# One-hots of the sources' places: made once per chunk of edges and fetched from DRAM in each step, in a graph network's counts loop

## The reference, cut to what matters

```python
h = relu(layernorm(x)); x = x + L0(h)    # mean of h[src] over each dst, then a dense layer
h = relu(layernorm(x)); x = x + L1(h)    # three attention layers over the edges
h = relu(layernorm(x)); x = x + L2(h)    # mean, max, min, std of messages over each dst
h = relu(layernorm(x)); x = x + L3(h)    # twice: mean of h[src] over each dst, dense layers
```

## Time and profile before

| | |
|---|---|
| median of three runs | 6377.4 us (6375.4 to 6395.1) |
| profiled execution, its own time | 6355.5 us |
| its span | 6353.5 us |
| busy: PE, DVE, ACT, POOL | 41%, 57%, 42%, 69% of the span |
| counts loop, from its first one-hot | 106.6 to about 1041 us |

### The profile page before, as it was taken

One profiled execution on the slowest core, in us unless ns is written; L12 is line 12 of the kernel. 1 busy time (PEld: TensorE's weight loads), 2 busy tenths in 40 slices (PEclk: granted clock), 3 DMA queues, 4 the chain that ended last, 5 costly groups with the idle time before them and its releaser, 6 DMA issues.

```text
span 6353.5 us, 74225 instructions
## 1 busy us (share of the span) xinstructions
PE 2619.9 (41%) x16765; PEld 1698.8 (27%) x16765; DVE 3628.2 (57%) x10270; ACT 2647.2 (42%) x7239; POOL 4376.2 (69%) x4752
## 2 busy tenths in 40 slices
PE   2666666844444434434443344444310000001799
PEld 1111112433333323333333333333200000000444
DVE  4666666956666665566666566666655555555410
ACT  2444442056666635666662566666311111111200
POOL 3999995067777767777775777777477787876000
PEclk9999999866777766777775677777555555555899
DMA  2222224323333333333332333333246555555266
GB/s 87 87 88 87 88 87 175 134 81 111 111 111 111 110 87 93 110 110 110 110 110 79 99 111 110 111 110 110 64 177 224 208 215 217 216 218 195 82 217 228
DMA packets 322843, 824.24 MB, mean 130 GB/s; under 512 B 87854, under 2 KB 234266, under 8 KB 307806
## 3 DMA queue, kind: packets, MB, share of 16 engines
q1 hardware_dynamic: 220462, 600.45, 24.9%
q0 software_dynamic: 102192, 221.85, 14.7%
HBM read 360.65 MB, written 461.39 MB: 129 GB/s over the span
## 4 chain that ended last, share of the span: by engine, by line
POOL 48%; issue 15%; DMA 10%; PE 9%; DVE 9%; ACT 8%; SPq 1%; DVEq 0%; ACTq 0%; POOLq 0%
POOL big L604 32%; POOL big L563 15%; DMA big<-table,src_win 9%; ACT hT L734 5%; PE psT L847 5%; ACT big L760 1%; PE psY L1031 1%; PE psY L1001 1%; PE psY L949 1%; DVE lane_x L1265 1%; DVE far_b L1444 1%; ACT hT L740 1%; DVE top_b L1447 1%; DMA big<-A_d 1%; DVE big L1490 1%
## 5 line engine op out<-in xcount | busy, mean ns | idle before, releaser
L604 POOL DMA_INDIRECT big<-table,src_win x2968 | 3251.2, 1095 | 969.4 <-issue 848.8
L963 PE MATMUL psY<-big,hT 128*128 128x140 bf16 x12600 | 1216.0, 269 | 1752.9 <-ACT hT L740 1750.3
L963 PEld LDWEIGHTS psY<-big,hT 128*128 128x128 bf16 x12600 | 1061.8, 120 | 1907.5 <-ACT hT L740 1773.4
L734 ACT ACTIVATE hT<-src_bc,node_c 128x128 bf16<-128x128 f16 x4200 | 1292.9, 389 | 70.4 <-DMA src_bc<-pe_src_d 70.1
L563 POOL TENSOR_SCALAR big<-big 128x128 bf16<-128x128 bf16 x1584 | 931.8, 606 | 12.2 <-ACT big L664 12.2
L1479 DVE SCALAR_TENSOR_TENSOR big<-big,keep_win 128x132 f32<-128x132 f32 x2184 | 781.9, 358 | 78.5
L1486 DVE SCALAR_TENSOR_TENSOR big<-big,keep_win 128x256 f32<-128x256 f32 x784 | 374.9, 478 | 555.6 <-ACT big L760 527.9
L740 ACT ACTIVATE hT<-hT 128x640 bf16<-128x640 bf16 x840 | 590.6, 722 | 0.0
L1434 DVE TENSOR_TENSOR e_b<-big 128x56 f32<-128x56 f32 x168 | 36.7, 218 | 886.4 <-DMA big<-table,src_win 877.2
L759 ACT ACTIVATE big<-big 128x896 f32<-128x896 f32 x112 | 106.4, 950 | 984.3 <-DMA big<-table,src_win 984.3
L752 ACT ACTIVATE cw_b<-d_b 128x60 f32<-128x60 f32 x168 | 42.5, 253 | 1079.2 <-DVE d_b L1458 1079.2
(11 more groups left out here) (299 smaller groups left out, 3483.3 us busy)
## 6 DMA issues: line engine op xcount, KB each, us to landing
rows<-big SPq DMA_DIRECT2D x112, 1792.0 KB
rows<-big SPq DMA_DIRECT2D x168, 952.0 KB
big<-A_d SPq DMA_DIRECT2D x18, 6400.0 KB, 19.6
A_d<-big SPq DMA_DIRECT2D x396, 200.0 KB, 1.9
big<-table,src_win POOLq DMA_INDIRECT x2968
src_bc<-pe_src_d SPq DMA_DIRECT2D x168, 32.0 KB
table<-big SPq DMA_DIRECT2D x15, 350.0 KB
big<-A_d SPq DMA_DIRECT2D x3, 1600.0 KB, 6.9
```

Of the source, the lines that this page charges most:

```text
L604: pool.indirect_dma_start(out=rows[:, k, p.gather_at:p.gather_at + p.table_w], out_offset=None, in_=table, in_offset=bass.IndirectOffsetOn ...
L734: ins = nc.scalar.activation(is_src[:, t, P:P + n], src_bc[:, s % 2, 0:n], ACT.Square, bias=node_c[:, t:t + 1], scale=-1.0)
L963: ins = nc.tensor.matmul(psY[k][:, 0:p.table_w], is_src[:, t, k * P:(k + 1) * P], table_s[:, t, c, 0:p.table_w], start=(t == 0 and c == 0) ...
```

## The change

- POOL's loop L557 to L564 goes, with `loT`, the four transposes L892 per group and ACT's copies L664.
- A new tensor in DRAM, `lo_d`, holds the `hot_l` of every chunk: 196 x 128 partitions x 512 bf16, 25.7 MB. DVE makes them in a new part `places`, between `path` and `weights`: 50 instructions, each for up to four chunks, into a ring of three buffers that lie in `hT`. SP stores each batch, and a buffer is made anew when its store has landed.
- For this PE transposes the places directly from `edge_s` (8 matmuls, ahead of the marks), and ACT copies them to `lo_e`. The float16 identity is made earlier.
- `path` also turns the chunk's number of each step to integers, `chunk_row`.
- When all batches are stored, SP fetches the `hot_l` of the first four steps. In each step of its loop, behind the store of A, it reads the chunk's number of the step four further on into a register and issues the fetch of 128 KB into the buffer that is now free. A round of the loop has 12 steps. PE waits for the fetch's semaphore and no longer for POOL.

```diff
+MADE, CB = 3, 4
+        lo_d = nc.dram_tensor("lo_d", (nC, P, GJ * P), BF16).ap()
+        batches = [(a, c, min(CB, CP - c)) for a in range(2) for c in range(0, CP, CB)]
...
             sp.wait_ge(blk_rdy, 1)
-            with sp.Fori(0, STEPS // STATES, 1) as rnd:
-                for z in range(STATES):
-                    sp.wait_ge(state_rdy, rnd * STATES + (z + 1))
-                    to = sp.value_load(blk[0:1, bass.ds(rnd * STATES + z, 1)], min_val=0, max_val=DUMP + STEPS - 1)
+            for k, (a, c, n) in enumerate(batches):
+                sp.wait_ge(made, k + 1)
+                sp.dma_start(lo_d.rearrange("(c a) p w -> a p c w", a=2)[a, :, c:c + n, :],
+                             hot_c[:, k % MADE, 0:n, :, :].rearrange("p c j w -> p c (j w)")).then_inc(made_out[k % MADE], 16)
+            for z in range(MADE):
+                sp.wait_ge(made_out[z], 16 * len(range(z, len(batches), MADE)))
+            sp.wait_ge(chunk_row_rdy, 1)
+
+            def load_hots(t, z):
+                frm = sp.value_load(chunk_row[0:1, t], min_val=0, max_val=nC - 1)
+                sp.dma_start(hot_l[:, z, :, :], lo_d[bass.ds(frm, 1), :, :].rearrange("c p (j w) -> p (c j) w", j=GJ)
+                             ).then_inc(hot_l_in[z], 16)
+
+            for t in range(HOTS):
+                load_hots(slice(t, t + 1), t)
+            turn = STATES * HOTS // 2
+            with sp.Fori(0, STEPS // turn, 1) as rnd:
+                for i in range(turn):
+                    z = i % STATES
+                    sp.wait_ge(state_rdy, rnd * turn + (i + 1))
+                    to = sp.value_load(blk[0:1, bass.ds(rnd * turn + i, 1)], min_val=0, max_val=DUMP + STEPS - 1)
                     sp.dma_start(A_d[bass.ds(to, 1), :, :].rearrange("b p q -> p (b q)"),
                                  state_a[:, z, :]).then_inc(state_out[z], 16)
+                    load_hots(bass.ds(rnd * turn + (i + HOTS), 1), i % HOTS)
+            for z in range(HOTS):
+                sp.wait_ge(hot_l_in[z], 16 * (STEPS // HOTS + 1))
...
-            pool.wait_ge(const_rdy, 9)
-            pool.wait_ge(loT_rdy, 4)
-            for t in range(STEPS):
-                if t >= HOTS:
-                    pool.wait_ge(conv_ps, t - HOTS + 1)
-                for j in range(GJ):
-                    ins = pool.tensor_scalar(hot_l[:, t % HOTS, j, :], iota_l, loT[:, j, t:t + 1], None, ALU.is_equal)
-                ins.then_inc(hot_p, 1)
...
+            for a in range(2):
+                act.wait_ge(lo_ps, a + 1)
+                nc.scalar.copy(lo_e[:, a, :, :], psC[2 + a][:, 0:GJ * CP].rearrange("p (j c) -> p j c", j=GJ)).then_inc(lo_rdy, 1)
             deviations(0)
             normalize(0)
-            for k in range(4):
-                act.wait_ge(loT_ps, k + 1)
-                nc.scalar.copy(loT[:, :, k * P:(k + 1) * P],
-                               psT[1][:].rearrange("p (j t) -> p j t", j=GJ)).then_inc(loT_rdy, 1)
...
             for t in range(STEPS):
-                pe.wait_ge(hot_p, t + 1)
                 pe.wait_ge(hot_v, t + 1)
+                pe.wait_ge(hot_l_in[t % HOTS], 16 * (t // HOTS + 1))
...
+                dve.wait_ge(blk_rdy, 1)
+                link(v.tensor_scalar(blk_t, chunk1, -1.0, None, ALU.add))
+                v.tensor_copy(chunk_row, blk_t).then_inc(chunk_row_rdy, 1)
...
+            def places():
+
+                dve.wait_ge(lo_rdy, 2)
+                for k, (a, c, n) in enumerate(batches):
+                    if k >= MADE:
+                        dve.wait_ge(made_out[k % MADE], 16 * (k // MADE))
+                    v.tensor_tensor(hot_c[:, k % MADE, 0:n, :, :],
+                                    iota_l.unsqueeze(1).unsqueeze(1).broadcast_to([P, n, GJ, P]),
+                                    lo_e[:, a, :, c:c + n].rearrange("p j c -> p c j").unsqueeze(3).broadcast_to([P, n, GJ, P]),
+                                    ALU.is_equal).then_inc(made, 1)
...
             fields()
             path()
+            places()
             weights()
```

More of the change, by code:

```diff
@@ L250, in build @@
         T_c = words(32 * G + QW // 2 + P // 2 + 16, 4)
-        assert 33 * G <= SIDE
+        chunk_row = words(33 * G, G).bitcast(I32)
+        lo_e = words(34 * G, nC * GJ // 2).bitcast(BF16).rearrange("p (a j c) -> p a j c", a=2, j=GJ)
+        assert 34 * G + nC * GJ // 2 <= SIDE
+        hot_c = hT[:].rearrange("p t n -> p (t n)")[:, 0:MADE * CB * GJ * P // 2].bitcast(BF16).rearrange(
+            "p (z c j w) -> p z c j w", z=MADE, c=CB, j=GJ)
+        batches = [(a, c, min(CB, CP - c)) for a in range(2) for c in range(0, CP, CB)]
         hot_q = words(0, HOTS * GJ * QW // 2).bitcast(BF16).rearrange("p (z j q) -> p z j q", z=HOTS, j=GJ)
@@ L256, in build @@
         qT = words(TAB, 4 * G).rearrange("p (j t) -> p j t", j=GJ)
-        loT = words(TAB + 4 * G, 4 * G).rearrange("p (j t) -> p j t", j=GJ)
         assert TAB + 8 * G <= U
@@ L322, in build @@
         marks_rdy, mark_ps, chunk_rdy, chunk_ps = sem("marks_rdy"), sem("mark_ps"), sem("chunk_rdy"), sem("chunk_ps")
+        ident_rdy = sem("ident_rdy")
         blk_rdy, c_rdy, edge_t_in = sem("blk_rdy"), sem("c_rdy"), sem("edge_t_in")
-        q_rdy, qT_ps, loT_ps, qT_rdy, loT_rdy = sem("q_rdy"), sem("qT_ps"), sem("loT_ps"), sem("qT_rdy"), sem("loT_rdy")
-        hot_v, hot_d, hot_s, hot_p = sem("hot_v"), sem("hot_d"), sem("hot_s"), sem("hot_p")
+        q_rdy, qT_ps, qT_rdy = sem("q_rdy"), sem("qT_ps"), sem("qT_rdy")
+        lo_ps, lo_rdy, made, chunk_row_rdy = sem("lo_ps"), sem("lo_rdy"), sem("made"), sem("chunk_row_rdy")
+        made_out = [sem(f"made_out{z}") for z in range(MADE)]
+        hot_l_in = [sem(f"hot_l_in{z}") for z in range(HOTS)]
+        hot_v, hot_d, hot_s = sem("hot_v"), sem("hot_d"), sem("hot_s")
         conv_ps, state_rdy = sem("conv_ps"), sem("state_rdy")
@@ L863, in _ @@
             pe.wait_ge(const_rdy, 9)
+            pe.wait_ge(edge_rdy, 3)
+            pe.wait_ge(ident_rdy, 1)
+            for a in range(2):
+                for j in range(GJ):
+                    ins = nc.tensor.matmul(psC[2 + a][:, j * CP:(j + 1) * CP], edge_s[0:CP, a, 2, j * P:(j + 1) * P],
+                                           ident_h[0:CP, 0:CP], start=True, stop=True)
+                ins.then_inc(lo_ps, 1)
             pe.wait_ge(marks_rdy, 1)
@@ L1136, in path @@
                 dve.wait_ge(const_rdy, 9)
+                v.tensor_copy(ident_h[:], ident[:]).then_inc(ident_rdy, 1)
                 link(v.tensor_copy(pos[:, 0:2], part_i[0].rearrange("p (a e) -> p a e", a=2)[:, :, 0]))
@@ L1143, in path @@
                 ins.then_inc(marks_rdy, 1)
-                v.tensor_copy(ident_h[:], ident[:])
                 dve.wait_ge(mark_ps, 1)
```

## The result

The changed kernel took 6532.7 us (median of four runs, 6524.7 to 6547.5) against 6386.3 us for the kernel before (four runs, 6375.4 to 6401.4): 1.023 times as long, 95% interval 1.020 to 1.026. The forecast was 6557 us, slower than before; the measured time is 24 us under it and inside the range. The profiled execution took 6528.45 us, 172.9 more than that of before (1.027 times).

What follows compares the result with a forecast made beforehand. POOL bounds the loop at 2.353 us a step, and SP would after the change. Prelude 109, loop 70 and tail 1 make +180 us: 6536 us profiled, 6557 us with 22 added for the median; range 6473 to 6638.

Steps and rivals of the forecast that it cites:

- SP's turn bounds the loop: In the counts loop, SP's instructions take 2.53 us a step against POOL's 2.353: 70 us longer over 396 steps.
- The first half: SP's existing work in each loop step: wait, block's number into a register, store of A; 1.32 us.
- the second: SP's added work in each loop step: chunk's number into a register and the fetch's DMA instruction; 1.21 us.
- the loop's tail: Behind the loop SP also waits for the last fetch: about 1 us.
- The prelude: Ahead of the loop, DVE makes and SP stores all chunks' one-hots: the loop starts 109 us later, bounds 76 and 124.
- The conversion to the median: On the whole time: the 22 us between profiled execution and median of before, added to 6536 to give 6557 us.
- Rival (a): In the loop, SP is not the bound and DVE is next at 1.5 us a step: 6148 us; chance 0.09.
- Rival (b): In SP's loop, register loads take 470 ns in both halves, 2.93 us a step: +339, 6716 us; chance 0.04.
- Rival (c): SP bounds the loop at 2.38 us a step or less, with fast batches ahead: +87, 6465 us; chance 0.06.

Runs made afterwards that it cites:

- run 1: The changed kernel with the loop's fetch always taking chunk 0, so no chunk number is loaded into a register: 6283.1 us, 1.88 us a step.
- run 2: The changed kernel with each fetch in the loop taking 32 KB instead of 128, register load and DMA instruction kept: 6517.0 us, 2.50 us a step.
- run 7: The kernel before plus SP's chunk-number register load and an 8 KB DMA in each step: 7724.5 us against 7702.0 on that chip, 2.52 us a step.
- run 9: The kernel of run 3 plus one unused register load in each of SP's turns: 6291.1 us, 1.99 us a step.
- run 10: The kernel of run 3 with the loads of src_i and dst_i moved behind the stores of the one-hots on SP: 6032.7 us, 0.9495 of the kernel before.
- run 3: The changed kernel with POOL instead of SP issuing the fetch, as an indirect DMA: 6055.9 us, 0.952 of the kernel before, 1.37 us a step.
- run 4: The kernel before with POOL doing one of its four comparisons in each step from the fifth on: 5954.3 us, 1.37 us a step.

## Why the prediction held, point by point

- **SP's turn bounds the loop.** Right. The step predicted was 2.53 us, measured 2.50. The first half was priced at 1.32, wake-up and branch of every six steps included, the second at 1.21; a plain turn took 1.26 and 1.18, and the branch and single longer turns add 0.06. Runs 1, 2, 7 and 9 show the cause: take the register load out and the step falls with the bytes unchanged, take bytes out and it stays, put the half into the kernel before and SP's waits vanish, add a load and the step rises by 0.62 us. The term was +71 us with the loop's tail and came out at 58.7: the shorter turn is worth some 11 us, and PE starts 0.84 us after the first one-hot where it took 2.62 with POOL.
- **The prelude.** Predicted +109, measured +110.1. Batches 2.28 us, DVE waiting from 57.7 to 90.19 (predicted 58 to 91), the batches' end at 193.4 (192), then the 15 and 8 us whose cover was gone. That the first store is late by the loads of `src_i` and `dst_i` is shown by run 10: with them out of the way it left SP at 53.4 instead of 72.85 and landed 4.9 us later instead of 17.3. That the second part is one DMA engine's backlog is read from the earlier trace rows, not tested by itself. Of the two rows between which the batch's price was chosen, L1468 gave the right number, 1.1 ns an element, but it could not show the reason. It is a float32 row, and the kernel before has a float32 sum of two inputs read straight that is as slow, 396 elements in 0.57 us (L1151, below). With 0.15 us fixed that is 1.06 ns an element, and L1468's is 1.05. So L1468 is explained by its type alone, and the choice of the slow rate for a bf16 batch was supported by no row. The Trainium skill (VectorE: DVE Perf Modes, "Mode 2×_1P — pack two bf16 into one 32-bit read") supports it, since a repeated element is no step of one; the trace agrees with 2284 ns for 2048 bf16 elements. The batch also compares where the faster bf16 row takes a minimum, so no run here separates the repetition from the operation. Of the kernel before:

```profile
47.47 0.57 DVE L1151 TENSOR_TENSOR big<-big 128x396 f32<-128x396 f32 x1
```

- **The conversion to the median.** This is the step with most of the miss. The sum on the profiled execution gave 6536 us and that execution took 6528.5. (The two smaller misses offset each other in part: the loop's term came out 12 us too large, the prelude 1 us and the part behind the loop 4 us too small.) To it I added the 22 us by which the median of before stood over its profiled execution; the changed kernel's median stands 4 over its own. On the two other chips with the same late stages the kernel before had medians of 6358.1 and 6354.7, about its profiled 6355.5. So the profile was no exception; the four runs on record with the result were high, for a reason that stays open. Against 6355 or so the change costs about 175 us and not 146.
- **Rival (a), DVE next at 1.5 us, 6148 us.** Rightly a rival, since SP had to be shown; but its price was wrong. DVE's one-hots take 318 to 328 ns when POOL is out of the way (362 beside it), and the next bound is 1.3 to 1.37, not 1.5. Run 3 gives what the change could have been worth with the fetch on an idle engine: 6056 us.
- **Rival (b), longer register loads.** Not in the changed kernel: 269 ns median, 278 at most for the block's number. The Trainium skill (DMA: Bandwidth & Descriptors, "Latency and other measured facts") names about 600 ns as the least; 269 ns here says otherwise. Longer loads do occur in other runs: up to 931 ns where the DMA engines were 79% busy (run 3), 355 ns in the median at 56% (run 1), but also 67 over 300 ns at 41% in run 4, while the changed kernel had none in its loop at 40%. So the busy DMA engines that the rival gave as its reason are not shown to be it.
- **Rival (c), SP bound but short.** Neither its 2.38 us a step nor its fast batches came.

## What to carry to other kernels

A queue that only issues DMAs has a turn like any engine, and the busy table does not show it: take the time between two of its waits less the wait itself, and add to it every register load (0.6 us with its register work here) and every DMA instruction (0.34 to 0.43 us here) of a change before believing that a freed engine frees the loop. If a fetch needs an address out of memory in each step, give it to an idle engine; here that turned +2.3% into -4.8%. And work moved ahead of a loop costs its own time (here 112 us of DVE) and, on top, what its stores wait behind somebody else's loads (31 us here, by run 10): look at when the queue comes to the first store, not only at the bytes.

## What the runs showed that I had not expected

- A register load out of SBUF on SP takes 262 to 269 ns and is as long in the median at 79% DMA share (270), but single ones then last up to 931 ns; in run 1 the median itself was 355. In run 4 nearly all the long ones are the first behind the branch of SP's loop, in run 1 none of these is long. What makes a load long is open.
- A DMA instruction with a fixed address took SP 433 ns, one with an address from a register 338.
- The loop's 400-column matmuls took 533 ns on average at a granted clock of 1.00, 523 at 0.51, and 339 at 0.98 in run 3, where PE is busy 61% of the stretch (64% before). The granted clock of the row alone did not tell how fast they went; what did is open.
